# A four-layer residual stack on one core: the convolution kernel's product cut into 64 small matmuls, the third layer's transposes moved forward, and one more weight block turned by VectorE

## What is computed

```
x = x + L0(x)   # state space layer: y = conv(x * mask, K) + D x, K = 2 Re(Cs exp(dtA l)), l = 0..1023
x = x + L1(x)   # x W1^T plus a low-rank part, gated by a top-2 choice over 8 experts
x = x + L2(x)   # x W2^T plus one of five low-rank parts
x = x + L3(x)   # x Wq^T, Wq: W3 plus its low-rank delta, quantised to a sorted codebook of 64
```

## Time and profile before

| | |
|---|---|
| median of 3 runs | 995.47 us (992.75 to 996.88) |
| profiled execution, its own time | 991.54 us |
| its span | 989.7 us |
| TensorE busy | 974.8 us, 98% |
| VectorE busy | 842.5 us, 85% |
| ScalarE busy | 456.2 us, 46% |
| GpSimd busy | 281.1 us, 28% |
| granted clock of TensorE, mean | 0.999 |

### The profile page before, as it was taken

One profiled execution on the slowest core, in us unless ns is written; L12 is line 12 of the kernel. 1 busy time (PEld: TensorE's weight loads), 2 busy tenths in 40 slices (PEclk: granted clock), 3 DMA queues, 4 the chain that ended last, 5 costly groups with the idle time before them and its releaser, 6 DMA issues.

```text
span 989.7 us, 16510 instructions
## 1 busy us (share of the span) xinstructions
PE 974.8 (98%) x4705; PEld 786.5 (79%) x4705; DVE 842.5 (85%) x1651; ACT 456.2 (46%) x862; POOL 281.1 (28%) x346
## 2 busy tenths in 40 slices
PE   9999999999999999999999999999999999999997
PEld 5465559877878788888888888888888888888886
DVE  6799999999955789888988888888888888889863
ACT  3342426252755554454544554445545445454531
POOL 6510000766344323222233222332222322223200
PEclk9999999999999999999999999999999999999999
DMA  8814010101113356645455455565555655556421
GB/s 292 128 27 86 0 43 1 43 1 19 25 22 67 60 91 117 104 90 106 91 110 107 92 104 95 105 112 93 99 98 97 117 98 97 99 96 116 80 43 43
DMA packets 370485, 82.05 MB, mean 83 GB/s; under 512 B 343170, under 2 KB 363586, under 8 KB 370450
## 3 DMA queue, kind: packets, MB, share of 16 engines
q1 hardware_dynamic: 369442, 80.90, 43.1%
q10 hardware_dynamic: 1008, 0.76, 0.3%
HBM read 60.88 MB, written 20.71 MB: 82 GB/s over the span
## 4 chain that ended last, share of the span: by engine, by line
PE 76%; ACT 1%; issue 1%; DVE 1%; DVEq 0%; ACTq 0%
PE bank L789 35%; PE bank L1024 10%; PE bank L776 7%; PE bank L755 5%; PE bank L810 5%; PE bank L766 4%; PE bank L744 4%; PE bank L780 4%; PE bank L816 1%; PE bank L800 1%; PE bank L805 0%; PE bank L794 0%; PE bank L986 0%; PE bank L1013 0%; PE bank L975 0%
## 5 line engine op out<-in xcount | busy, mean ns | idle before, releaser
L789 PE MATMUL bank<-Mh,strips_r 128*128 128x512 f32 x1020 | 289.1, 395 | 0.0
L789 PEld LDWEIGHTS bank<-Mh,strips_r 128*128 128x128 f32 x1020 | 189.9, 188 | 40.9
L1101 ACT ACTIVATE SK<-ZZ 64x448 f32<-64x448 f32 x128 | 73.9, 577 | 214.2 <-DVE ZZ L1458 211.9
L550 POOL TENSOR_TENSOR Cl<-QC,Ch 128x256 fp32r<-128x256 f32 x32 | 39.1, 1223 | 449.7 <-ACT Ch L1083 449.7
L789 PE MATMUL bank<-Ml,strips_r 128*128 128x512 f32 x510 | 159.9, 395 | 0.0
L1458 DVE SCALAR_TENSOR_TENSOR ZZ<-ZZ,coef 128x192 f32<-128x192 f32 (+1 forms) x256 | 106.9, 457 | 10.1 <-DVE ZZ L1449 0.3
L789 PEld LDWEIGHTS bank<-Ml,strips_r 128*128 128x128 f32 x510 | 95.9, 188 | 22.6
L956 PE MATMUL bank<-E,A 128*128 128x512 f32 (+1 forms) x320 | 97.8, 466 | 0.0
L1449 DVE SCALAR_TENSOR_TENSOR ZZ<-ZZ,coef 128x384 f32<-128x384 f32 (+1 forms) x128 | 79.9, 624 | 13.5 <-DVE ZZ L1458 6.7
L956 PEld LDWEIGHTS bank<-E,A 128*128 128x128 f32 x320 | 51.0, 191 | 44.9 <-issue 44.4
L776 PE MATMUL bank<-Ml,strips_r 128*128 128x296 f32 x256 | 70.7, 299 | 0.0
(11 more groups left out here) (319 smaller groups left out, 1863.1 us busy)
## 6 DMA issues: line engine op xcount, KB each, us to landing
X<-in_x SPq DMA_DIRECT2D x256, 64.0 KB, 2.6
XT<-in_x SPq DMA_DIRECT2D x256, 64.0 KB, 2.5
out_x<-O SPq DMA_DIRECT2D x62, 256.0 KB, 3.3
toep<-kpad SPq DMA_DIRECT2D x128, 64.0 KB, 2.2
E<-in_L_cond_W SPq DMA_DIRECT2D x8, 512.0 KB, 9.3
vq<-in_L_cond_weight SPq DMA_DIRECT2D x8, 512.0 KB, 3.7
turned<-TB SPq DMA_DIRECT2D x29, 128.0 KB, 2.3
Bt<-turned SPq DMA_DIRECT2D x116, 32.0 KB, 2.2
```

Of the source, the lines that this page charges most:

```text
L789: pe.matmul(psO[nh][:, :], xs[:, c, :], ms[:, c, nh * BANK:(nh + 1) * BANK], start=(c == 0 and n == 0), stop=False)
L1101: act.activation(SK[ri * N:(ri + 1) * N, hh, :].rearrange("p (c b) -> p c b", b=B), ZZ[hh * N:(hh + 1) * N, :, ri, :], ACT.Copy).then_inc( ...
```

## The change

It has three parts.

1. W2_BY_PE becomes 2: block 2 of W2 is loaded in 128-byte runs by four DMAs in place of one, and turned by VectorE before the quantising begins; its eight transposes and two copies go away.
2. The a3 jobs of the next quarter stand one m job earlier, after m(q,2), m(q,4), m(q,6) and m(q,7). In the last quarter the first tile's state work stands one m job earlier too, ScalarE's state columns and `Vt` halves with it, and VectorE computes C1 and C2 before it waits for m(3,0).
3. The kernel product is made by 64 matmuls, one for each head, with four stationary columns (the head's C1) and 32 moving columns (the head's powers), in front of m(3,4). The output of head 4g + a lies in partitions 32a to 32a+3. The transposes and `Kt` go away. D is added by VectorE in PSUM in four instructions, `Kh` and `Kl` are made in four instructions each of 4 x 512 elements, and stored by four DMAs each.

```diff
-        W2_BY_PE = 3
+        W2_BY_PE = 2
-        order += deltas(0) + first_two(5, 6) + [("w2t", 2, 0), ("w2t", 2, 1)] + first_two(7)
+        order += deltas(0) + first_two(5, 6, 7)
-                if q + 1 < QUARTERS and mt in (3, 5, 7, 8):
-                    order += [("a3", q + 1, (3, 5, 7, 8).index(mt))]
+                if q + 1 < QUARTERS and mt in (2, 4, 6, 7):
+                    order += [("a3", q + 1, (2, 4, 6, 7).index(mt))]
-        KERN_IN = 5
+        KERN_IN = 4
...
-                sp.dma_start(Drow[:, :], D_skip.rearrange("(a h) -> a h", a=1)).then_inc(ld_d, 16)
+                for a in range(PARTS):
+                    sp.dma_start(Drow[a * SPAN:a * SPAN + 1, :], D_skip.rearrange("(a h) -> a h", a=1)).then_inc(ld_d, 16)
...
-                    sp.wait_ge(ready, 1)
-                    sp.dma_start(bass.AP(kpad.tensor, part * KP + P, [[2 * KP, H], [1, P]]), t[:, :].bitcast(F32)).then_inc(kpad_stored, 16)
+                    for a in range(PARTS):
+                        sp.wait_ge(ready, a + 1)
+                        sp.dma_start(bass.AP(kpad.tensor, 2 * KP * a + part * KP + P, [[SPAN, PARTS], [2 * KP * PARTS, H // PARTS], [1, SPAN]]),
+                                     t[a * SPAN:a * SPAN + PARTS, :].rearrange("p (g r) -> p g r", r=SPAN).bitcast(F32)).then_inc(kpad_stored, 16)
...
-                    for g in range(part * H // 16, (part + 1) * H // 16):
-                        heads = slice(4 * g, 4 * g + 4)
-                        last = pe.matmul(bank[2][:, 16 * g:16 * (g + 1)].rearrange("p (h k) -> p h k", k=PARTS),
-                                         Vt[:, heads, :].rearrange("p h r -> p (h r)"), X1T[:, heads, 0:PARTS], start=True, stop=True)
+                    for g in range(H // PARTS):
+                        for a in range(PARTS):
+                            last = pe.matmul(bank[2][a * SPAN:a * SPAN + PARTS, g * SPAN:(g + 1) * SPAN], X1T[:, PARTS * g + a, 0:PARTS],
+                                             Vt[:, PARTS * g + a, :], start=True, stop=True)
+                    last.then_inc(kern_full, 1)
...
-                    if j == ("m", LAST_Q, 3):
+                    if j == ("m", LAST_Q, 2):
                         state_transpose(0, first=True)
-                    elif j == ("m", LAST_Q, 4):
+                    elif j == ("m", LAST_Q, 3):
                         for hh in range(HB):
                             chunk_states(0, hh, first=True)
                     elif j == ("m", LAST_Q, 5):
-                        kern_transpose()
                         state_transpose(1)
...
+                            act.wait_ge(kf_ready, PARTS)
+                            for a in range(PARTS):
+                                rows = slice(a * SPAN, a * SPAN + PARTS)
+                                act.activation(Kh[rows, :], bank[2][rows, :], ACT.Copy).then_inc(kh_ready, 1)
...
+                w2_turn(2)
                 n_kept = dve.value_load(n_steps[0:1, 0:1], min_val=0, max_val=K_CODES - 1 - FIXED)
...
+                dve.wait_ge(kern_full, 1)
+                dve.wait_ge(ld_d, 16 * PARTS)
+                for a in range(PARTS):
+                    first = bank[2][a * SPAN:a * SPAN + 1, ::SPAN]
+                    dve.scalar_tensor_tensor(first, first, 1.0, Drow[a * SPAN:a * SPAN + 1, a::PARTS], ALU.add, ALU.add).then_inc(kf_ready, 1)
                 dve.wait_ge(cols_ready, 1)
                 for level in range(2):
                     carry(0, level)
                     carry_across(0, level)
-                dve.wait_ge(kern_taken, 4)
-                dve.wait_ge(ld_d, 16)
-                dve.scalar_tensor_tensor(Kt[0:1, 0, :], Kt[0:1, 0, :], 1.0, Drow[:, :], ALU.add, ALU.add).then_inc(kf_ready, 1)
+                for a in range(PARTS):
+                    rows = slice(a * SPAN, a * SPAN + PARTS)
+                    dve.wait_ge(kh_ready, a + 1)
+                    dve.tensor_tensor(Kl[rows, :], bank[2][rows, :], Kh[rows, :].bitcast(F32), ALU.subtract).then_inc(kl_ready, 1)
                 for level in range(2, len(LEVELS)):
                     carry(0, level)
                     carry_across(0, level)
```

More of the change, by code:

```diff
@@ L125, in resid_stack_kernel @@
     mrow = place("mrow", [P, MULT], F32)
-    Drow = place("Drow", [1, H], F32)
+    Drow = place("Drow", [P, H], F32)
     half_pi = place("half_pi", [P, 1], F32)
@@ L172, in resid_stack_kernel @@
     Bt = place("Bt", [P, HB, P], F32)
+    Kh = place("Kh", [P, H // PARTS * SPAN], F32R)
+    Kl = place("Kl", [P, H // PARTS * SPAN], F32R)
     assert cursor[0] <= at_expo
@@ L219, in resid_stack_kernel @@
     Cl = place("Cl", [P, HB, P], F32R)
-    Kt = place("Kt", [SPAN, PARTS, H], F32)
     assert cursor[0] <= at_quant3 + 4 * QCOLS
@@ L976, in a3, with kern @@
                         ps[:, m * P:(m + 1) * P], qq[q][:, m % QT_TILES, (2 * n + m // QT_TILES) * P:(2 * n + m // QT_TILES + 1) * P], ident[:, :]))
[L978 to L983, removed]
-                    for g in range(part * H // 16, (part + 1) * H // 16):
-                        heads = slice(4 * g, 4 * g + 4)
-                        last = pe.matmul(bank[2][:, 16 * g:16 * (g + 1)].rearrange("p (h k) -> p h k", k=PARTS),
-                                         Vt[:, heads, :].rearrange("p h r -> p (h r)"), X1T[:, heads, 0:PARTS], start=True, stop=True)
-                    if part == 3:
-                        last.then_inc(kern_full, 1)
-                def kern_transpose():
-                    pe.wait_ge(kf_ready, 1)
-                    for k in range(PARTS):
-                        last = pe.transpose(bank[3][0:H, k * SPAN:(k + 1) * SPAN], Kt[:, k, :], ident[0:SPAN, 0:SPAN])
-                    last.then_inc(kernT_full, 1)
+                def kern():
+                    pe.wait_ge(cols_ready, 3)
+                    pe.wait_ge(tab_out, 1)
+                    pe.wait_ge(m_taken, M_LAST)
+                    for g in range(H // PARTS):
[3 more added lines that the diff above has]
+                    last.then_inc(kern_full, 1)
                 def m(q, mt):
@@ L1021, in m @@
                         lhs = QT[:, kt, mt * P:(mt + 1) * P]
-                        if (q, mt) == (LAST_Q, KERN_IN) and kt < 4:
-                            kern(kt)
+                        if (q, mt, kt) == (LAST_Q, KERN_IN, 0):
+                            kern()
                         last = pe.matmul(m_bank(n)[:, 0:QO], lhs, A3[q % 2][:, kt, :], start=(kt == 0), stop=(kt == NC - 1))
@@ L1198, in state_columns, with kernel_rows @@
                     last.then_inc(cols_ready, 1)
-                def kernel_rows():
-                    act.activation(Vt[lo_n, :, :], pow_r[lo_n, :, 0:SPAN], ACT.Copy)
-                    act.activation(Vt[hi_n, :, :], pow_i[hi_n, :, 0:SPAN], ACT.Copy).then_inc(cols_ready, 1)
+                def kernel_rows(part):
+                    rows, power = ((lo_n, pow_r), (hi_n, pow_i))[part]
+                    act.activation(Vt[rows, :, :], power[rows, :, 0:SPAN], ACT.Copy).then_inc(cols_ready, 1)
                 lo_n, hi_n = slice(0, N), slice(N, 2 * N)
@@ L1348, in _ @@
                             sines(1)
+                        elif j == ("m", LAST_Q, 0):
+                            state_columns()
                         elif j == ("m", LAST_Q, 1):
[L1350 to L1351 removed]
                             for hh in range(HB):
                                 x_hi(0, hh, first=True)
[L1354 removed]
+                            kernel_rows(0)
+                        elif j == ("m", LAST_Q, 2):
+                            b_hi(0, first=True)
+                            kernel_rows(1)
                         elif j == ("m", LAST_Q, 3):
[L1356 removed]
+                            states_in(0, first=True)
                         elif j == ("m", LAST_Q, 4):
[L1358 to L1363 removed]
+                            act.wait_ge(kf_ready, PARTS)
+                            for a in range(PARTS):
+                                rows = slice(a * SPAN, a * SPAN + PARTS)
+                                act.activation(Kh[rows, :], bank[2][rows, :], ACT.Copy).then_inc(kh_ready, 1)
                         elif j == ("m", LAST_Q, 5):
                             c_hi(0, first=True)
[L1366 to L1367 removed]
                             states_out(0, range(HB), first=True)
@@ L1848, in read @@
                     dve.wait_ge(m_full, mno["m", LAST_Q, mt] + 1)
-                read(0)
-                for hh in range(HB):
-                    turn_q(0, hh, first=True)
                 tc = [P, H, PARTS]
@@ L1862, in _ @@
                 dve.tensor_tensor(C2, C2, spare, ALU.subtract).then_inc(tab_out, 1)
+                read(0)
+                for hh in range(HB):
+                    turn_q(0, hh, first=True)
                 read(2)
```

24 lines of the change are left out of this document (4 added, 20 removed).

## The result

Of these two kernels in one set of runs, the one after takes 988.01 us in the median (986.27 to 989.59, five executions), the one before 995.47 us: a ratio of 0.9927 with an interval of 0.9908 to 0.9947. The profiled execution of after takes 988.01 us as well, with a span of 986.2 us where before had 989.7: only 3.5 us shorter. So two questions stand: why the spans differ by more than 2.4 us, and why the medians differ by twice what the spans do.

What follows compares the result with a forecast made beforehand. TensorE was taken as the bound, busy 974.8 of 989.7 us. Terms -0.2 - 1.3 - 1.6 + 0.7 = -2.4 us gave a median of 993.1 us, with an 8-in-10 range of 989 to 998 us.

Steps and rivals of the forecast that it cites:

- The size of part 3: Kernel product: 4.0 us of matmuls and transposes go, 128 passes at 37 ns come, 4.7 us; 0.7 us more.
- The second rival: Kernel product nearly free by overlapping column groups: 1.0 us, -3.0 us for part 3, total -6.1 us, 989.4 us; chance 0.15.
- the lower bound of the term: Kernel product: time goes with moving columns as in BW, one eighth of 62.5 ns a pass, 1.0 us.
- Boundary 2 to 3: Wait before m(3,0), set by GpSimd's diagonal: a3(3,3) moved ahead of BW removes it, gain 1.6 us.
- The comparisons that wait for VectorE do time m(0,9): Before m(0,9): VectorE, through ScalarE's comparisons and BW copy, sets its start, 207.64 us; TensorE waits 3.2 us.
- ScalarE's extra copy: Boundary 0 to 1: ScalarE copies a3(1,3) ahead of BW, which puts m(0,9) back by 0.47 us.
- VectorE's 0.2 us: Part 1: VectorE's added 1.25 us transpose fills a 1.04 us wait, delaying its chain and m(0,9) by 0.2 us.
- The block is in time: W2's block 2 most likely lands at 30 to 31 us, just in time for VectorE's transpose at 31.8 us.
- the 0.87 us of TensorE: Part 1: eight transposes saved at 39 us only turn into a longer wait at 207 us.
- -0.2, -1.3, -1.6 and +0.7: Terms in us for boundaries 0 to 1, 1 to 2, 2 to 3 and the kernel product; sum -2.4 us.
- The clock, the fourth rival: Behind the wait before m(0,9), clock falls to 1.2 GHz for one m job: +3.5 us, total +1.1 us, 996.6 us; chance 0.05.
- The carry-over to the median: Whole run: the -2.4 us worked out on the 991.54 us profiled execution is applied to the 995.47 us median, 993.1 us.

Runs made afterwards that it cites:

- k_order: After with the loops over g and a swapped, so 16 matmuls in a row write the same 32 partitions; 990.32 us, ratio 0.9953.
- f_diag: After with the last quarter's a3 jobs in the order 3, 0, 1, 2; 986.72 us, ratio 0.9917.
- f_fill: After with 28 spare transposes of the identity on TensorE ahead of m(0,9); 986.4 us, ratio 0.9921.
- f_cmp: After with ScalarE's four last-quarter comparisons moved from behind m(0,4) to m(0,7) to behind m(1,0) to m(1,3); 983.29 us, ratio 0.9891.
- u_w2: After with part 1 undone: block 2 of W2 loaded whole and transposed by TensorE again; 986.28 us, ratio 0.9926.
- f_both: After with the four comparisons moved and the last quarter's a3 jobs in the order 3, 0, 1, 2; 982.26 us, ratio 0.9889.
- f_both_u_w2: f_both with part 1 undone, block 2 of W2 transposed by TensorE; 982.9 us (982.75 to 983.19).
- c_before2: Before, unchanged, profiled again, one execution; 995.92 us at a mean clock of 0.995.
- c_before3: Before, unchanged, profiled once more, one execution; 992.47 us at a mean clock of 0.997.
- the later set: After, unchanged, timed once more beside before; 988.29 us, seven executions, ratio 0.9954, with before's median at 992.23 us.
- b_fill: Before with 16, 6, 12 and 20 spare transposes ahead of m(0,9), m(1,0), m(2,0), m(3,0); 992.53 us, ratio 1.0001; copies 992.04 and 992.22 us.
- o_kern: Before with part 1, part 2's moved a3 jobs, the moved comparisons and the a3 order 3, 0, 1, 2; old product kept; 984.98 us, ratio 0.9923.
- u_w2_a3: After with part 1 undone and the a3 jobs back in their old places; 991.27 us, ratio 0.9971.
- c_before: Before, unchanged, as a control; 993.7 us (992.14 to 997.02), ratio 0.9997; its profiled execution took 993.49 us.

## Why the prediction was wrong, step by step

**The size of part 3, the step that failed first.** The prediction took 37 ns for a pass, from the loads in the earlier trace rows, and made it +0.7 us. It measured 9.7 ns. Product and transposes of before cost 4.0 us, the new product costs 1.2 us: -2.8 us. The second rival, "the product is nearly free, because its four column groups overlap", was true, and its 1.0 us was the lower bound of the term. The argument that set it aside, that a backlog of instructions carries only so far, was not in any row, and 256 instructions in a row show none of it. BW's 0.59 us of loads were divided by 16 and taken for a pace, but the loads follow the passes there, which come every 62.5 ns. k_order shows that the turns over the groups are the cause. The Trainium skill (page "TensorE: Matmul & The Clock Gate", section "Wait — 56ns, not 53.3ns?") gives 25 ns as the least time from start to start, and 62 ns with decoding by microcode; 27.8 ns within one column group lies near the first, and the 9.7 ns across groups lies below both, so here the measurement decides.

**Boundary 2 to 3.** Predicted -1.6 us, with GpSimd's diagonal at its 0.86 us of the earlier trace rows. Moved forward, the same two additions take 3.49 us. VectorE's exponent work still runs there until 279.4 us, as this row of after's VectorE shows:

```profile
277.69 1.69 DVE L1834 TENSOR_TENSOR theta<-theta,expo 128x1344 f32<-128x1344 f32 x1
```

In before the additions started at 279.60 us, when VectorE was done. A duration was carried to a place with another neighbour. f_diag has them done long before (they start at 260.37 us there, and take 3.26 us), and the wait is gone: their end is what held m(3,0). That it is VectorE that slows them is read from the overlap, and wasn't tried. The earlier trace rows had the warning: the same two additions took 4.23 us a quarter earlier. So the move gave 0.6 us (by f_fill, below), and 1.0 us of the forecast stayed as a wait of 1.1 us.

**What held.** The comparisons that wait for VectorE do time m(0,9), as predicted (207.64 us predicted, 207.45 us measured; m(1,0) 208.1 and 208.21 us), and f_cmp shows it by taking them away. Of the two terms, only one arrived: ScalarE's extra copy (0.47 us). VectorE's 0.2 us is there at 33 us but not at the comparisons, which start at 196.26 us where before had 196.27 us. The block is in time: its four DMAs take SP's queue 14.4 us, and VectorE turns it at 31.84 us and adds from 33.01 us (31.8 and 33.0 us predicted).

```profile
196.26 2.00 ACT L1227 ACTIVATE above<-vq,fixed_tau 128x2048 uint8<-128x2048 f32 x1 [7.47 <-DVE vq L1765]
```
```profile
12.65 14.40 SPq L418 DMA_DIRECT2D W2s<-in_L_cond_W  x4
```
```profile
31.84 1.25 DVE L1683 STREAM_TRANSPOSE A<-W2s 128x1024 f32<-128x1024 f32 x1
33.01 2.58 DVE L1764 TENSOR_TENSOR vq<-vq,dq 128x1024 f32<-128x1024 f32 x2
```

So the 0.87 us of TensorE are absorbed (u_w2: 0 at equal clock; f_both against f_both_u_w2: 0.6 us once nothing absorbs them). No wait is left at m(2,0) nor at `within(0)`.

**The sum without any fall** can be read from f_fill, where the clock doesn't fall before the end, against the profiled execution of before. Its span is 984.7 us, 5.0 us less. By its marks, before against f_fill: m(1,0) at 208.26 and 208.03 us, -0.2; m(2,0) at 244.25 and 242.50 us, another -1.5; m(3,0) at 280.56 and 278.21 us, another -0.6; the first tile's line 776 (779 in f_fill) at 324.53 and 319.60 us, another -2.6; behind it -0.1 us. Predicted were -0.2, -1.3, -1.6 and +0.7. That the two spans differ by 3.5 us, near the 2.4 us predicted, is in part luck: the product came out 3.5 us better than its term and m(3,0) 1.0 us worse, and after's fall takes 1.5 us of the 5.0 us back.

**The clock, the fourth rival, was true as well.** It was given 0.05, because the present wait of 1.69 us showed a clock of 1.00. But one execution at 1.69 us bears out nothing for 3.03 us, nor even for other executions: c_before2 has a wait of 1.89 us there, with a fall behind it. Ten of after's twelve executions have a mean clock of 0.998 or less and take 987.8 us or more; f_fill has none. Its price was taken too high, as a whole m job at half pace (+3.5 us): the clock is back after 3.4 us, and costs 1.7 us. The Trainium skill (page "TensorE: Matmul & The Clock Gate", section "What's actually happening") has the idle engine fall to half clock, and the trace of after agrees; the second fall of c_before2, with TensorE busy, is not of that kind. The clock falls behind m(0,9) in before too, in c_before2 and c_before3. But there m(2,0) still waits for ScalarE and GpSimd, and this wait gives a part back. From the start of m(1,0) to that of m(1,9) c_before3 takes 1.3 us more than before, and the wait behind it is 0.82 us instead of 1.26; c_before2 takes 1.7 us more, and its wait is 0.38 us. Part 2 removed that wait, so nothing is left there to take up after's loss.

**The carry-over to the median**, 995.47 minus the difference of the traces, failed for this reason. The profiled execution of before (991.54 us, clock 0.999) is of its lowest heap; the median of its set was of the highest, and the one execution of that heap with a trace (c_before2) has the fall in the old product. At equal clock the change is worth 992.06 - 986.46 = 5.6 us, which rests on after's two executions and agrees with the 986.4 us of f_fill. The medians of the first set lie 995.47 - 992.06 = 3.4 us and 988.01 - 986.46 = 1.6 us above that: 5.6 + 3.4 - 1.6 = 7.4 us, where the medians differ by 7.5. In the later set before's median lies 0.2 us above its lowest heap and after's 1.8 us: 5.6 + 0.2 - 1.8 = 4.0 us. So how many executions of each kernel fall is part of the measured gain. With the waits filled or removed, five of the 20 executions with the old product (b_fill with its two copies, o_kern) are at 0.996 or less, and none of the 17 with the new one (f_fill, f_cmp, f_both, f_both_u_w2). That speaks for the new product falling less often; it doesn't show that it never does.

**Open.** Three of after's twelve executions take 989.6 us at 0.995 to 0.997, and u_w2 (989.86) and u_w2_a3 (992.8 and 993.2) have such ones too. By the mean clock they spend 6 to 10 us at half pace (0.003 or 0.005 x 986 x 2), some of it perhaps after TensorE's last work. No trace caught one, so where is not known. They may have two falls of 3.4 us, or one of 6.8 us in or near the new product: 986.5 + 3.3 = 989.8 us fits as well, so that the new product has no such fall is not shown. Why before falls in the product in some executions and not in others isn't known either.

## What to carry to other kernels

Read the mean clock of every execution before a profiled time is set beside a median: the same two kernels were 7.5 us apart and then 3.9 us, by how many executions of each fell, and 5.6 us at equal clock. A wait that grows costs more than its length when TensorE's clock falls behind it, and a wait further on may have hidden part of that cost until one removes it; filling the wait with spare work, or better, moving the work that makes it (here four comparisons of ScalarE's, 986.4 to 983.3 us at equal clock), gives it back and more. Before a duration is moved to another place, look at what runs beside it there. Small matmuls like these should take turns over the four column groups.

## What the runs showed of the hardware

- 128 float32 passes with four stationary and 32 moving columns take 1.24 us in turns over the column groups (9.7 ns each, with their loads) and 3.56 us (27.8 ns) with 16 matmuls in a row in one group.
- The granted clock fell to 0.50 while TensorE was busy without a gap: in sets of eight passes with 16 moving columns, 0.96 us a set, between passes of 256 columns. It stayed there for 6.8 us and cost 3.3 us, in the one execution of c_before2; the three other traces of this kernel (before, c_before, c_before3) don't have it, and what makes it is not shown.
- Behind a wait of 3.03 us (2.79 us in c_before) it fell for 3.4 us and cost 1.4 to 1.7 us; 28 spare transposes in the wait kept it at 1.00 (f_fill). It also fell behind waits of 1.70, 1.89 and 1.92 us at the same place (u_w2_a3, c_before2, c_before3), and not behind those of 1.69, 1.73 and 2.19 us (before, c_before, u_w2).
- GpSimd's two 128x128 additions took 0.86 us when VectorE was idle (before) and 3.26 us (f_diag), 3.49 us (after) and 4.23 us (before, a quarter earlier) when it ran; that VectorE is the reason is not tested.
